# Cross-attention on one core: the statistics of four sequences first, loads held back behind the first weights, and a new order of the steps before the first scores

## The reference

```python
mu = jnp.mean(input, axis=(1, 2), keepdims=True)
var = jnp.var(input, axis=(1, 2), keepdims=True)
xn = (input - mu) * jax.lax.rsqrt(var + EPS)
xn = xn * gamma[None, :, None] + beta[None, :, None]
q = jnp.einsum('oc,ncs->nos', Wq, xn) + bq[None, :, None]
kv = jnp.einsum('od,nds->nos', Wkv, context) + bkv[None, :, None]
...
att = jax.nn.softmax(jnp.einsum('nhqc,nhkc->nhqk', q * scale, k * scale), axis=-1)
y = jnp.einsum('nhqk,nhkc->nhqc', att, v)
...
out = jnp.einsum('co,nos->ncs', Wo, y) + bo[None, :, None]
return input + out
```

## Time and profile before

| what | value |
|---|---|
| three runs, median (lowest, highest) | 228.94 us (227.13, 229.73) |
| profiled execution, span from first to last instruction | 228.2 us |
| mean granted TensorE clock in it | 0.965 |
| busy: PE, DVE, ACT, POOL | 208.6, 199.3, 181.1, 160.3 us |
| first score product (L522) starts | 28.0 us |

### The profile page before, as it was taken

The page is one execution under the profiler, slowest core; times in us unless marked ns, Lnnn a source line. Parts: engine busy times, 40 slices in busy tenths (PEclk is TensorE's granted clock), DMA queues, the critical chain, the costliest instruction groups (busy, mean ns, idle before and its releaser), DMA issues.

```text
span 228.2 us, 7194 instructions
## 1 busy us (share of the span) xinstructions
PE 208.6 (91%) x2511; PEld 179.9 (79%) x2511; DVE 199.3 (87%) x589; ACT 181.1 (79%) x371; POOL 160.3 (70%) x157
## 2 busy tenths in 40 slices
PE   6968878799999999999999998999999999999872
PEld 6857757588888798889888887888888888887761
DVE  3589987879898999899999999999999998989765
ACT  2374586787889988898889888989897979888880
POOL 5135185777987877789788887789686869776460
PEclk9975897999999999999999999999999999999998
DMA  5964137480767566566665665656657656442000
GB/s 134 261 272 93 27 82 174 107 184 14 164 141 160 131 153 142 132 141 151 140 153 122 160 151 121 151 127 154 142 127 166 149 133 143 93 94 62 13 3 23
DMA packets 31090, 29.04 MB, mean 127 GB/s; under 512 B 4240, under 2 KB 29840, under 8 KB 31056
## 3 DMA queue, kind: packets, MB, share of 16 engines
q1 hardware_dynamic: 30224, 28.07, 52.4%
q10 hardware_dynamic: 832, 0.53, 1.0%
HBM read 3.80 MB, written 1.05 MB: 21 GB/s over the span
## 4 chain that ended last, share of the span: by engine, by line
PE 41%; POOL 20%; issue 13%; ACT 11%; DVE 11%; ACTq 2%; POOLq 0%; DVEq 0%
POOL p_lo L773 19%; PE ps_sc L522 6%; PE ps_max L546 6%; PE ps_sc L523 5%; PE ps_z L479 4%; ACT p_full L678 4%; DVE neg_max L894 4%; ACT p_hi L675 3%; PE ps_z L481 3%; PE ps_z L480 3%; PE ps_z L414 3%; PE ps_m L589 2%; PE ps_t L497 2%; PE ps_m L590 2%; DVE z_sum L910 2%
## 5 line engine op out<-in xcount | busy, mean ns | idle before, releaser
L773 POOL TENSOR_TENSOR p_lo<-p_full,p_hi 128x512 f16<-128x512 f32 x122 | 139.9, 1163 | 42.3 <-ACT p_full L678 41.2
L675 ACT ACTIVATE p_hi<-ps_sc 128x512 f16<-128x512 f32 x128 | 77.9, 608 | 18.3 <-PE ps_sc L523 15.9
L894 DVE TENSOR_REDUCE neg_max<-ps_max 128x2 f32<-128x512 f32 x128 | 85.9, 677 | 6.9 <-PE ps_max L546 6.8
L678 ACT ACTIVATE p_full<-ps_sc 128x512 f32<-128x512 f32 x128 | 78.7, 615 | 0.0
L522 PE MATMUL ps_sc<-t_a,c_seq 128*128 128x256 f32 x256 | 71.2, 300 | 3.5 <-issue 2.6
L523 PE MATMUL ps_sc<-t_b,c_seq 65*128 65x256 f32 x256 | 67.3, 284 | 0.0
L479 PEld LDWEIGHTS ps_z<-u_hi,p_hi 128*128 128x128 f16 x512 | 46.4, 97 | 12.8 <-issue 8.2
L479 PE MATMUL ps_z<-u_hi,p_hi 128*128 128x65 f16 x512 | 53.0, 195 | 2.2 <-DVE p_lo L930 1.9
L522 PEld LDWEIGHTS ps_sc<-t_a,c_seq 128*128 128x128 f32 x256 | 49.2, 192 | 5.9 <-issue 4.6
L480 PE MATMUL ps_z<-u_lo,p_hi 128*128 128x64 f16 x512 | 52.8, 193 | 0.0
L481 PE MATMUL ps_z<-u_hi,p_lo 128*128 128x65 f16 x512 | 52.7, 194 | 0.0
(11 more groups left out here) (108 smaller groups left out, 233.9 us busy)
## 6 DMA issues: line engine op xcount, KB each, us to landing
t_a<-t_a SPq DMA_DIRECT2D x90, 128.0 KB, 2.4
t_b<-t_b SPq DMA_DIRECT2D x30, 128.0 KB, 2.5
x_seq<-x_hi SPq DMA_DIRECT2D x15, 128.0 KB, 2.4
c_pad<-c_hi SPq DMA_DIRECT2D x30, 64.0 KB, 2.1
c_seq<-c_hi SPq DMA_DIRECT2D x15, 128.0 KB, 2.4
x_res<-x_tiles SPq DMA_DIRECT2D x4, 256.0 KB, 6.7
out<-x_res SPq DMA_DIRECT2D x16, 64.0 KB, 2.0
x_seq<-x_lo SPq DMA_DIRECT2D x15, 64.0 KB, 2.1
```

What stands on the lines that cost most here:

```text
L675: nc.scalar.activation(p_hi[:, buf, :, :].rearrange("p t s -> p (t s)"), scores, ACT.Exp).then_inc(act_phi, 1)
L678: nc.scalar.activation(p_full[:, head % 2, :], scores, ACT.Exp).then_inc(act_p, 1)
L773: nc.gpsimd.tensor_tensor(p_lo[:, buf, :, :].rearrange("p t s -> p (t s)"), p_full[:, head % 2, :], p_hi[:, buf, :, :].rearrange("p t s -> ...
L894: nc.vector.tensor_reduce(to, ps_max[:, unit % 2, :].rearrange("p (t s) -> p t s", t=KT), X, ALU.max, negate=True).then_inc(dve_max, 1)
```

## The change

Statistics are no longer taken from `x_res` but from `x_raw`, in which each partition half holds another sequence, so a block-diagonal `mean_w` (now set by DVE) replaces the full one. They come in two groups: group 0 (the pairs 0 and 1, four sequences) before the weights are folded, group 1 (six pairs) during heads 1 to 3, with its mean and variance products placed in front of the value products of heads 0 and 4 of sequence 0 in a spare part of `ps_z`. The square root, its table of functions and the reciprocal are replaced by Ln and Exp from one table. POOL finishes the factors of group 1 (seven small instructions at step 12) and DVE normalises the first pair instead of POOL. SP loads two pairs of x, the first pair of context and the weights first, and only after the first weights have landed (`dma_qk`) the rest, `x_res` last. The tops and the bound move from `ps_sc` to `ps_m` and to later steps; the scaling of B's maximum and the bias `bo2` move into step -5; the copies of B move to step -4. The fourth turn of t goes to `ps_t` instead of `ps_sc`.

```diff
-T_FIRST = (0, 0, 2, 3, 4, 4, 4, 5, 6, 6, 6, 6, 7, 7, 7, 7, 8, 8, 8, 8, 8, 9, 9, 9, 10, 10)
-T_LO_FIRST = (0, 0, 0, 1, 2, 3, 4, 4, 5, 6, 6, 6, 6, 6, 6, 7, 8, 8, 8, 8, 8, 9, 9, 9, 9, 9)
+T_FIRST = (0, 0, 2, 3, 3, 4, 4, 5, 6, 6, 6, 6, 7, 7, 7, 7, 8, 8, 8, 8, 8, 9, 9, 9, 10, 10)
+T_LO_FIRST = (0, 0, 0, 0, 1, 2, 3, 4, 5, 6, 6, 6, 6, 6, 6, 7, 8, 8, 8, 8, 8, 9, 9, 9, 9, 9)
-MAX_FIRST = (0, 0, 2, 4, 4, 5, 6, 7, 9, 10, 11, 13, 15, 16, 17, 19, 20, 20, 22, 23, 24, 24, 26, 28, 28, 29)
+MAX_FIRST = (0, 0, 2, 4, 4, 6, 8, 8, 9, 10, 11, 13, 15, 16, 17, 19, 20, 20, 22, 23, 24, 24, 26, 28, 28, 29)
-U_FIRST = (2, 3, 7, 8)
-MT_FIRST = (-3, 1, 6)
+U_FIRST = (3, 4, 7, 8)
+MT_FIRST = (-4, 1, 6)
-TOP_AT, UNSCALE_AT, B_LOW_AT = -5, -1, 1
-TOPS_AT, BOUND_AT = -6, -4
+BTOP_AT, TOP_AT, UNSCALE_AT, B_LOW_AT = -5, -2, 0, 1
+B_COPY_AT, TOPS_AT, BOUND_AT = -4, -3, -1
+STATS_AT, MEAN_WITH, VAR_WITH, ROOT_AT, NORM_AT = (1, 2, 3), (0, 0), (0, 4), 11, 12
+X_LOADS = ((0, 2), (2, 4), (4, 8))
+X_GROUPS = ((0, 2), (2, 8))
...
-            return (ps_t[:], ps_z[:, 0], ps_z[:, 1], ps_sc[:, 0], ps_t[:], ps_z[:, 0])[turn] if turn < T_EARLY else ps_t[:]
+            return (ps_t[:], ps_z[:, 0], ps_z[:, 1], ps_t[:], ps_t[:], ps_z[:, 0])[turn] if turn < T_EARLY else ps_t[:]
...
-            return (0, 0, 0, 0, 1, 2, 5)[turn] if turn <= T_EARLY else turn
+            return (0, 0, 0, 1, 4, 2, 5)[turn] if turn <= T_EARLY else turn
...
+            load_x(0)
+            load_c(0)
+            sp.dma_start(w_sb[0:C, 0:W_BO], w_in[:, 0:W_BO]).then_inc(dma_w, 16)
+            sp.wait_ge(dma_qk, 16 * 2)
+            load_c(1)
+            load_c(2)
+            load_x(1)
+            load_x(2)
             for c in range(N // CHUNK):
                 sp.dma_start(x_res[:, chunk(c), :], x_tiles_in[:, chunk(c), :]).then_inc(dma_xt[c], 16)
...
+            def variance(g):
+                first, end = X_GROUPS[g]
+                pe.wait_ge(dve_spread, g + 1)
+                pe.wait_ge(dve_q, g + 1)
+                moving = [t[:, first:end, a] for t in (spread, dev2) for a in range(2)]
...
-            pe.wait_ge(pool_const, 4)
+            pe.wait_ge(pool_const, 3)
+            pe.wait_ge(dve_const, 3)
             keep_warm(WARM_MEAN)
+            mean(0)
+            variance(0)
             pe.wait_ge(dma_qk, 16 * 2)
             products_a(0)
             products_a(1)
...
             pe.wait_ge(dma_w, 16)
             pe.wait_ge(dma_w_tail, 32)
             products_b()
-            keep_warm(WARM_T)
...
+                    if e == MEAN_WITH:
+                        mean(1)
+                    if e == VAR_WITH:
+                        variance(1)
...
+            def inverse_root(g):
+                first, end = X_GROUPS[g]
+                act.wait_ge(dve_var, g + 1)
+                nc.scalar.activation(log_var[:, first:end], var[:, first:end], ACT.Ln).then_inc(act_log, 1)
+                act.wait_ge(act_log, g + 1)
+                nc.scalar.activation(y0[:, first:end], log_var[:, first:end], ACT.Exp, scale=-0.5).then_inc(act_root, 1)
...
+            c_high(0)
+            a_highs(0)
+            inverse_root(0)
+            a_highs(1)
             act.wait_ge(dve_scale, 1)
...
+            statistics(*X_GROUPS[0])
+            spreads(0)
+            deviations(0)
             dve.wait_ge(act_c0, 1)
             nc.vector.tensor_tensor(c_seq[C:P, 0, 0, :], ctx_raw[0:C, 0, :], c_seq[0:C, 0, 0, :].bitcast(fp32), ALU.subtract).then_inc(dve_c0, 1)
+            variances(0)
...
+                if n * H + h == BTOP_AT:
+                    dve.wait_ge(pe_bw, 1)
+                    nc.vector.tensor_reduce(tops[0:C, 1:2], ps_sc[0:C, 1, :], X, ALU.max, apply_absolute_value=True).then_inc(dve_btop, 1)
...
+                if n * H + h in STATS_AT:
+                    part, (first, end) = STATS_AT.index(n * H + h), X_GROUPS[1]
+                    per = (end - first) // len(STATS_AT)
+                    statistics(first + part * per, first + (part + 1) * per)
```

More of the change, by code:

```diff
@@ L490, in step @@
                         pe.wait_ge(dve_alo, k // 2 + 1)
-                    if turn == 3:
-                        pe.wait_ge(dve_bo, 2)
                     need(pe, dve_tlo, t_bank_free(turn))
@@ L614, in c_high, with a_highs @@
                 nc.scalar.activation(c_hi[:, first:end, :], ctx_raw[:, first:end, :], ACT.Copy).then_inc(act_chi, 1)
-            for bank in range(2):
+            def inverse_root(g):
+                first, end = X_GROUPS[g]
+                act.wait_ge(dve_var, g + 1)
+                nc.scalar.activation(log_var[:, first:end], var[:, first:end], ACT.Ln).then_inc(act_log, 1)
+                act.wait_ge(act_log, g + 1)
+                nc.scalar.activation(y0[:, first:end], log_var[:, first:end], ACT.Exp, scale=-0.5).then_inc(act_root, 1)
+            def a_highs(bank):
                 act.wait_ge(pe_a, bank + 1)
@@ L688, in step @@
                     transpose_out(*e)
+                if n * H + h == B_COPY_AT:
+                    act.wait_ge(dve_btop, 1)
+                    for k in range(2):
+                        nc.scalar.activation(b_sb[k * C:(k + 1) * C], ps_sc[0:C, 1, :], ACT.Copy).then_inc(act_b, 1)
+                if n * H + h == ROOT_AT:
+                    inverse_root(1)
                 if n * H + h == B_HIGH_AT:
@@ L818, in _ @@
-            dve.wait_ge(pe_var, 1)
-            for k in range(2):
-                rows = slice(k * C, (k + 1) * C)
-                spread = ps_m[rows, 64:64 + 2 * N].rearrange("p (j k a) -> p k j a", k=2, a=2)
-                last = nc.vector.tensor_reduce(var[rows], spread[:, k], X, ALU.add)
-            chain(last)
-            nc.vector.tensor_scalar_add(var[:], var[:], EPS).then_inc(dve_var, 1)
-            a_low(0)
-            dve.wait_ge(act_root, 1)
-            chain(nc.vector.reciprocal(y0[:], root[:]))
@@ L841, in _, with statistics, spreads @@
-            for k in range(2):
-                rows = slice(k * C, (k + 1) * C)
-                nc.vector.tensor_tensor(bo2[rows], ps_sc[0:C, 0, BO_COL:BO_COL + 1], w_sb[0:C, W_BO:W_BO + 1], ALU.add).then_inc(dve_bo, 1)
-            a_low(1)
+            def statistics(first, end):
+                for j in range(first, end):
+                    loaded(dve, X_LOADS, dma_x, j)
+                    nc.vector.bn_stats(stats[:, j, :], x_raw[:, j, :]).then_inc(dve_stats, 1)
+            def spreads(g):
+                first, end = X_GROUPS[g]
+                dve.wait_ge(dve_stats, end)
+                nc.vector.tensor_scalar(spread[:, first:end, :], parts(g, 2), 1.0 / P, 0.0, ALU.mult, ALU.add).then_inc(dve_spread, 1)
```

236 lines of the change are left out of this document (142 added, 94 removed).

## The result

| | time, median (lowest, highest) | profiled span | mean granted clock |
|---|---|---|---|
| before, four runs on the same chip | 229.33 us (227.13, 230.47) | 228.2 us | 0.965 |
| changed, four runs | 235.41 us (234.21, 236.08) | 232.6 us | 0.949 |

The changed kernel takes 1.0359 times as long as the one before, with a 95% interval from 1.0273 to 1.0445: by the medians it is 6.1 us slower, where 3.6 were forecast.

What follows compares the result with a forecast made beforehand. PE was taken to set the pace from 60 us on, so only the opening could move. 3.0 us late at the sixteenth maximum, 0.4 variance and 0.2 POOL gave 3.6 over the 228.94 median: 232.5 us, range 227.8 to 235.4.

Steps and rivals of the forecast that it cites:

- The base: Starting time of the sum: the median of 228.94 us, 0.7 above the profiled span of 228.2.
- Statistics earlier: Opening: scale of x at 15.0 us, 0.8 earlier; context's maxima on DVE at 17.2 instead of 18.63, 1.45 earlier.
- The table of functions: Removing the second table load on ACT gains 0.1 us at most, already inside the 0.8 us of the earlier statistics.
- The first wait: DVE, maxima of heads 4 and 5: they wait for the fourth turn of t behind the first remainder, 0.8 us.
- The second wait: Sequence 1's turn waits for the fourth remainder, the bound behind it: 0.5 us turn plus 0.1, ACT has it at 29.7.
- ACT's way to the scaled B: ACT's unchanged list after the turn takes 3.75 us: scaled B ends at 33.45 instead of 30.77, 2.7 us later.
- To the sixteenth maximum: DVE after the scaled B: six statistics (2.1 us) and `spread` (0.15) add 0.3 net of idle time, 3.0 us late.
- Later statistics: Group 1's variance on PE costs 0.4 us (0 to 1.0), POOL's seven small instructions 0.2 (0 to 2).
- Milder: Rival: full clock at the first wait, fast transfer of sequence 1's maxima, variance and POOL hidden: 229.7 us; chance 0.23.
- Faster: Rival: DVE alone decides and never waits, both new waits under 0.2 us: 226.5 us; chance 0.14.
- Table: Rival: the drain behind the table load was real work ahead of x, 1.3 us more gained: 231.2 us; chance 0.06.
- Worse: Rival: half clock at the second wait too, DVE's idle time kept, POOL's factors delay `p_full`: 235.4 us; chance 0.12.

Runs made afterwards that it cites:

- e13: The kernel before with eight products of constants (16 records) added at PE's end: 229.91 us, ratio 1.0045.
- e14: The changed kernel with 12 warming products on PE instead of 16: 235.82 us, ratio 1.0307.
- e15: The changed kernel run again as it is, on another chip: 234.07 us against 228.06 for the kernel before, ratio 1.0275.
- e1: The kernel before with only the new order of steps and the fourth turn in `ps_t`, statistics and loads as before: 232.63 us against 229.13, ratio 1.0165.
- e3: The changed kernel with sequence 1's two turns issued one step later, so that the bound stands ahead of them: 233.43 us, ratio 1.0175.
- e4: The changed kernel without group 1's statistics, products and factors (scale 1, shift 0 for sequences 4 to 15): 232.01 us against 229.13, ratio 1.0117.
- e7: The changed kernel without SP's wait for the first weights, so context, x and `x_res` load at once: 234.54 us, ratio 1.0331.
- e11: The changed kernel with group 1's statistics at steps 5 and 6 instead of 1, 2 and 3: 237.81 us, ratio 1.048.
- e12: The changed kernel with three more warming products on PE between the mean and the variance: 234.43 us, ratio 1.033.
- e8: Old order and banks with the new statistics and loads, eight warming products, B's maximum and bias ahead of the context's maxima: 231.65 us, ratio 1.019.
- e10: e8 with group 1's statistics left out (scale 1, shift 0): 228.96 us, ratio 1.002, on another chip.

## Why the prediction was wrong, point by point

The sign, the two waits, their places and the place of the loss were right. The sum was 2.5 us too small, and the forecast of 232.5 was 2.9 us below the 235.41 measured, which lies just above the range's end of 235.4. Of the 2.9, 1.1 are the base, 0.9 the time outside the span, and 0.8 the terms within it. By its own steps:

- **What bounds the kernel.** Right. PE sets the pace from 60 us on, and the offset does not grow after head 32.
- **The base.** The failed step is "against the median". I set the profiled span of 228.2 beside the median of 228.94 and took 0.7 us as what lies around a span, where it is 1.8. All later runs of before lie 1.76 to 1.93 above their spans, so the execution shown took about 230.0 us and was a slow one of its kind. One reason shows in e13, which is the same program up to its end: there the transfer of sequence 1's maxima landed after 2.44 us instead of 3.93, and head 8 came 0.9 us earlier although head 0 came 0.65 later. Differences against the execution shown understate the loss against the median by some 1 us.
- **Outside the span.** No term at all. The changed kernel's profiled run took 2.72 us more than its span (235.32 and 232.6), so 0.9 us of the loss lie there (e13 and e14 leave the cause open). In e15's job the same split comes from the medians of runs: spans 231.1 against 226.2 us, 4.9 in the span, and 1.1 outside.
- **In the span: 4.4 us instead of 3.6.** Together: 230.0 + 4.4 + 0.9 = 235.3, the profiled run.
- **Statistics earlier.** The mean at 8.11 (forecast 8.2), A at 11.87 (11.8) and the root at 13.54 (13.5) were right. The eight small DVE instructions took 1.93 us and not 1.5, since two of one column cost 0.45: the scale of x at 15.50 instead of 15.0, the maxima at 17.64 instead of 17.2.
- **The table of functions.** Its removal shows nowhere: the gain in front of the context's maxima was 1.0 us, less than forecast without it. The row of 1.28 us with 0.1 on the path was the right guide, and by the Trainium skill's 2.66 us (ScalarE: Activation LUTs, What ACT_TABLE_LOAD costs) the result would have been further off.
- **The first wait.** 1.16 us where 0.8 stood, and 1.16 to 1.21 in nine executions (changed kernel, e1, e3, e4, e7, e11, e12, e14, e15). Half clock was right; from the start of the turn at 24.52 to DVE's start at 26.13 it took 1.6 us instead of 1.4, of which the remainder covered 0.45 instead of 0.65.
- **The second wait.** Forecast as 0.5 for the turn and 0.1 to hand over. The turn ran at full clock as taken (its products follow at 0.12), but from the remainder's end at 30.13 to ACT's start at 31.02 there were 0.89 us, and DVE, with the bound behind the turn, waited 1.20. ACT had the turn at 31.02 instead of 29.7: 0.44 from the late maxima, 0.36 from the first wait, 0.3 from this one, 0.2 from small gaps. The full clock was luck: in five of nine executions with this wait the clock there was half, and the wait 1.89 us. e1 shows the wait without the new statistics, e3 the kernel without the wait.
- **ACT's way to the scaled B.** 3.88 us instead of 3.75. The scaled B ended 4.1 us late instead of 2.7.
- **To the sixteenth maximum.** The price of six statistics on DVE was right (2.2 us of work, of which idle time took most: 0.3 by head 8, by e4). The sixteenth maximum was 4.5 us late instead of 3.0, and 4.1 of this came from the late scaled B. The transfer of the maxima took 2.1 us instead of the 3.9 at which I had left it, and PE's own list reached the scores 0.9 us after it had landed. So sequence 1's scores were 3.2 us late, beside a forecast of 3.0: two errors of 1.5 us that cancelled, by luck. The length of this transfer belongs to the execution and not to the kernel: 3.93 and 2.44 with the program of before (the execution shown, e13), 2.08 and 2.66 with the changed one (shown, e15), 1.8 to 4.3 over all.
- **Later statistics.** The second failed step. I took 0.4 for the variance and 0.2 for POOL, with 0 and 1.0, 0 and 2 as bounds. e4 gives 1.2 and 0.5 (with 0.4 more at head 32 whose cause is open), e8 against e10 gives 0.8 and 0.5. The idle 1.76 us of 20 that were to cover the variance are not where it stands: PE had no idle time of 0.2 us from 48.5 to 53.5, and the value product behind the eight records started 0.81 us after the first of them. POOL's 27.4 us of idle time did not cover its seven instructions either: behind them it had no idle time of 0.2 us until 71.2, and PE waited 0.59 us for it.
- **Held-back loads.** Right, by e7.
- **The rivals.** "Milder" had the transfer right, but the clock was half at the first wait and the variance was not hidden; what I held against it, a half clock in the whole stretch before, was wrong, since before has 1.00 from 25 us on. "Faster" needed both waits under 0.2 us and falls by the first of them. "Table" needed a scale of x still earlier than forecast; it came 0.5 later. "Worse" gave the sum nearest to the result (235.4), but of its parts only half of POOL's was there in this execution. The half clock at the second wait was there in five others, among them e7, the changed kernel without the gate. DVE's idle time was not kept.

## What to carry to other kernels

When a step is moved down the list of a strict queue, write down every instruction that now stands behind it and who waits for the last of them: here a new order of the steps cost 3.5 us with nothing added (e1), moving one turn from ahead of the bound to behind it brought the scaled B forward by 1.7 (e3), and statistics moved two steps back on DVE stopped PE for 2.4 us. Idle time in a nearly full engine is no cover for new work on it unless the trace shows what ends that idle time, and that the new work fits ahead of it. Before a sum is set against a median, find out what the profiled execution itself took, and compare several executions: this opening moves by 1 us from one to the next, and one small transfer by up to 2. Look for the price of added work where the next engine waits, and not where the work stands: POOL's 2.1 us at 57.5 showed as 0.6 us of PE at 65.5.
